# Mixer, MLP and routed experts on one core: expert rows added to the output by an accumulating scatter, and two splits of weights moved

## What is computed

```python
x = x + mixer_and_mlp(layernorm(x))          # first block
x = x + experts(layernorm(x))                # second block

def mixer_and_mlp(x):
    h  = x + mamba2(rmsnorm(x, ln1_w))       # in-projection 512 -> 2576, conv, scan, out-projection 1024 -> 512
    h2 = rmsnorm(h, ln2_w)
    return h + silu(h2 @ gate_w) * (h2 @ up_w) @ down_w     # 512 -> 2048 -> 512

def experts(x):                              # 8 experts, width 352, the 2 best of each row
    w, idx = top_k(softmax(x @ Wr), 2); w = w / w.sum()
    return sum(w[k] * (silu(x @ Wg[idx[k]]) * (x @ Wu[idx[k]])) @ Wd[idx[k]] for k in range(2))
```

## Time and profile before

| what | before |
|---|---|
| median of 3 executions | 1528.81 us (1527.99 to 1529.47) |
| the profiled execution, its own time | 1526.85 us |
| its span in the trace | 1525.1 us |
| TensorE busy | 1444.7 us, 95% |
| VectorE busy | 775.2 us, 51% |
| ScalarE busy | 446.2 us, 29% |
| GpSimd busy | 447.2 us, 29% |
| mean granted clock of TensorE | 0.985 of full |

### The profile page before, as it was taken

One profiled execution on the slowest core, in us unless ns is written; L12 is line 12 of the kernel. 1 busy time (PEld: TensorE's weight loads), 2 busy tenths in 40 slices (PEclk: granted clock), 3 DMA queues, 4 the chain that ended last, 5 costly groups with the idle time before them and its releaser, 6 DMA issues.

```text
span 1525.1 us, 19801 instructions
## 1 busy us (share of the span) xinstructions
PE 1444.7 (95%) x6871; PEld 1052.3 (69%) x6871; DVE 775.2 (51%) x1235; ACT 446.2 (29%) x926; POOL 447.2 (29%) x497
## 2 busy tenths in 40 slices
PE   6799999889999998999999999999988999999996
PEld 4577778556666666888888888888867555555553
DVE  6969778699999992333333332333465221211211
ACT  4444445455555552212112121211121111111110
POOL 2402121257777662101011010101012233333332
PEclk9999999899999998999999999999999999999998
DMA  9123123622332225010000001200476122222220
GB/s 195 56 104 105 68 83 133 206 90 105 117 119 98 98 71 193 28 28 29 14 28 28 14 28 28 97 7 12 148 244 232 57 77 79 87 87 84 81 64 17
DMA packets 84978, 130.97 MB, mean 86 GB/s; under 512 B 29213, under 2 KB 45597, under 8 KB 84896
## 3 DMA queue, kind: packets, MB, share of 16 engines
q1 hardware_dynamic: 71488, 103.62, 21.0%
q0 software_dynamic: 9360, 25.18, 5.4%
q10 hardware_dynamic: 4048, 1.10, 0.3%
HBM read 91.59 MB, written 43.78 MB: 89 GB/s over the span
## 4 chain that ended last, share of the span: by engine, by line
PE 38%; DMA 15%; issue 4%; DVE 3%; ACT 0%; POOLq 0%; POOL 0%; DVEq 0%; ACTq 0%
PE fin_bank L1744 35%; DMA result_rows<-out_dram,idx 8%; DMA out_dram<-result_rows,idx 7%; DVE result_rows L1729 2%; PE fin_bank L1885 1%; PE fin_bank L1854 1%; PE fin_bank L1867 0%; PE fin_bank L1812 0%; PE fin_bank L1800 0%; DMA xs<-xn_rows,idx 0%; DVE ff_w_lo L1581 0%; PE fin_bank L1903 0%; DVE fi_bn L1616 0%; ACT ff_w_hi L1505 0%; PE fin_bank L1810 0%
## 5 line engine op out<-in xcount | busy, mean ns | idle before, releaser
L1744 PE MATMUL fin_bank<-ff_hT_hi,ff_w_hi 128*128 128x512 f32 x512 | 203.0, 397 | 3.2 <-DVE ff_w_lo L1551 3.2
L1744 PE MATMUL fin_bank<-ff_hT_hi,ff_w_lo 128*128 128x512 f32 x512 | 202.7, 396 | 0.0
L1744 PE MATMUL fin_bank<-ff_hT_lo,ff_w_hi 128*128 128x512 f32 x512 | 202.7, 396 | 0.0
L1885 PE MATMUL fin_bank<-wx,xT 128*128 x624 | 192.9, 462 | 1.0 <-ACT xT L1520 0.8
L1543 DVE TENSOR_TENSOR ff_prod<-ff_prod,fin_bank 128x512 f32<-128x512 f32 x64 | 44.0, 688 | 263.8 <-PE fin_bank L1744 263.8
L1388 POOL TENSOR_TENSOR ff_w_lo<-ff_stage,ff_w_hi 128x1024 fp32r<-128x1024 f32 (+1 forms) x24 | 56.5, 2354 | 411.7 <-ACT ff_w_hi L1495 406.9
L1885 PEld LDWEIGHTS fin_bank<-wx,xT 128*128 128x128 f32 x624 | 116.4, 192 | 60.0 <-issue 2.7
L1729 DVE SCALAR_TENSOR_TENSOR result_rows<-fin_bank,wt,result_rows 128x512 f32<-128x512 f32 x39 | 29.3, 751 | 234.6 <-DMA result_rows<-out_dram,idx 232.1
L628 PE MATMUL pj_bank<-hT_hi,w_in_hi 128*128 128x512 f32 x336 | 135.7, 404 | 11.8 <-DVE zst L548 8.7
L530 DVE SCALAR_TENSOR_TENSOR conv_acc<-raw,conv_w,conv_acc 128x512 f32<-128x512 f32 x144 | 113.2, 786 | 42.6 <-ACT raw L339 35.1
L628 PE MATMUL pj_bank<-hT_lo,w_in_hi 128*128 128x512 f32 x336 | 133.9, 398 | 0.0
(11 more groups left out here) (264 smaller groups left out, 2455.0 us busy)
## 6 DMA issues: line engine op xcount, KB each, us to landing
cv_rows<-cst SPq DMA_DIRECT2D x12, 1024.0 KB, 4.2
cv<-cv_rows SPq DMA_DIRECT2D x16, 768.0 KB, 4.3
zs_rows<-zst SPq DMA_DIRECT2D x8, 1024.0 KB, 6.5
zs<-zs_rows SPq DMA_DIRECT2D x16, 512.0 KB, 5.3
wx<-in_L_ffn_Wg_dram SPq DMA_DIRECT2D x8, 704.0 KB, 8.4
wx<-in_L_ffn_Wu_dram SPq DMA_DIRECT2D x8, 704.0 KB, 9.0
w_raw<-in_L_attn_in_proj_w_dram SPq DMA_DIRECT2D x32, 128.0 KB, 3.8
x<-_attn_hidden_states_dram SPq DMA_DIRECT2D x16, 256.0 KB, 5.6
```

Of the source, the lines that this page charges most:

```text
L1744: mm = eng.matmul(ps, w[a], x[b], start=first and i == 0, stop=last and i == 2)
L1885: mm = eng.matmul(ps[:, 0:EI], xT[j % 2][:, k, :], wx[:, bass.ds(e, 1), at:at + EI].rearrange("p a n -> p (a n)"), start=(k == 0), stop=(k ...
```

## The change

There are three edits.

**Experts.** The old rows of the output are no longer read. VectorE only multiplies the result by the weight into one of two buffers `rows`, and one indirect DMA per tile adds it to the output in DRAM (`compute_op=ALU.add`). Such a DMA may not name a row twice, nor leave one to chance, so the empty slots of a tile now name real rows that the tile doesn't hold, and add zero to them. Their numbers come from a second list, `put_idx`. VectorE works it out in 17 small steps, two wide ones (`oj`) and two wider ones (`onehot`), TensorE makes another table from it with 16 one-hot products, which stand in its list between `turn_x(1)` and the first `turn_width`, and VectorE finishes it after `product(0)` (`put_list`). Each accumulating DMA waits for the one before it. GpSimd's list is now: three gathers, the wait for the list, and then for each tile one gather ahead, the wait for the result, the wait for the last accumulation, and the accumulating DMA.

**Table load.** ScalarE runs an exponential of one column before it waits for data, which brings the load of its function table forward. In the first loop of ScalarE and of VectorE the order is turned round: the transposed rows of k come before the weights of k.

**Out-projection split.** The eight and eight instructions that split `wo_raw` go in two halves into gaps of chunk 0: on ScalarE behind `exps(0, 1)` and `exps(0, 2)`, on VectorE behind `score(0, 1)` and `score(0, 3)`. TensorE's first out-projection waits for the first four, its second for the rest.

```diff
         eng.activation(neg_cum[:, g, :], dtb[:, UPG * HEADS:2 * UPG * HEADS], ACT.Copy)\
            .then_inc(s["cum_done"], 1)
+    eng.activation(sp[:, 2, 0:1], ones[:, 0:1], ACT.Exp)
     eng.wait_ge(s["ln1_dma"], 16)
+    turned(0, 0)
     for k in range(KD):
+        if k + 1 < KD:
+            turned(0, k + 1)
         if k == 0:
             eng.wait_ge(s["wa_dma"], 32)
         split(k, 0, W_C)
-        turned(0, k)
...
     rows_in(0)
     norm_rows(0)
+    turned(0, 0)
     for k in range(KD):
+        if k + 1 < KD:
+            turned(0, k + 1)
         split(k + 1, k, 0, W_C)
-        turned(0, k)
...
+    def out_high(lo, hi):
+        if lo == 0:
+            eng.wait_ge(s["v_dma"], 16 * 9)
+            eng.wait_ge(s["wo_dma"], 16 * 4)
+        for n in range(lo, hi):
+            eng.activation(wo_hi[:, n, :], wo_raw[:, n, :], ACT.Copy, scale=normw[:, n:n + 1])\
+               .then_inc(s["wo_hi"], 1)
...
             exps(c, 1)
+        if c == 0:
+            out_high(0, HPG)
         if late:
             high(e, 1)
         if now:
             exps(c, 2)
+        if c == 0:
+            out_high(HPG, NB)
...
-        if c == 0:
-            eng.wait_ge(s["v_dma"], 16 * 9)
-            eng.wait_ge(s["wo_dma"], 16 * 4)
-            for n in range(NB):
-                eng.activation(wo_hi[:, n, :], wo_raw[:, n, :], ACT.Copy, scale=normw[:, n:n + 1])\
-                   .then_inc(s["wo_hi"], 1)
...
+    def out_low(lo, hi):
+        for n in range(lo, hi):
+            eng.wait_ge(s["wo_hi"], n + 1)
+            eng.scalar_tensor_tensor(wo_lo[:, n, :], wo_raw[:, n, :], normw[:, n:n + 1],
+                                     wo_hi[:, n, :].bitcast(F32), ALU.mult, ALU.subtract).then_inc(s["wo_lo"], 1)
...
             score(c, 1)
+        if c == 0:
+            out_low(0, HPG)
         if late:
             low(e, 1)
...
             score(c, 3)
+            if c == 0:
+                out_low(HPG, NB)
             decayed_c(c, 1)
...
-        if c == 0:
-            for n in range(NB):
-                eng.wait_ge(s["wo_hi"], n + 1)
-                eng.scalar_tensor_tensor(wo_lo[:, n, :], wo_raw[:, n, :], normw[:, n:n + 1],
-                                         wo_hi[:, n, :].bitcast(F32), ALU.mult, ALU.subtract).then_inc(s["wo_lo"], 1)
...
-        if e == 0 and a == 0:
-            eng.wait_ge(s["wo_lo"], NB)
+        if e == 0:
+            eng.wait_ge(s["wo_lo"], HPG * (a + 1))
...
-    for t in xs + [rows]:
+    for t in xs:
         eng.memset(t[:, :], 0.0).then_inc(s["cleared"], 1)
-    eng.wait_ge(s["cleared"], UN + 1)
+    eng.wait_ge(s["cleared"], UN)
     eng.wait_ge(s["ids"], 1)
-    def at(j):
-        return bass.IndirectOffsetOnAxis(ap=idx[:, j:j + 1], axis=0)
     def gather(j):
         if j >= UN:
             eng.wait_ge(s["xT_ps"], j - UN + 1)
-        eng.indirect_dma_start(out=xs[j % UN][:, :], out_offset=None, in_=dr["xn"], in_offset=at(j),
+        eng.indirect_dma_start(out=xs[j % UN][:, :], out_offset=None, in_=dr["xn"],
+                               in_offset=bass.IndirectOffsetOnAxis(ap=idx[:, j:j + 1], axis=0),
                                bounds_check=ROWS - 1, oob_is_err=False).then_inc(xs_s[j % UN], 16)
-    gather(0)
-    gather(1)
+    for j in range(3):
+        gather(j)
     eng.wait_ge(s["out_dma"], 16 * NR)
+    eng.wait_ge(s["ids"], 3)
     for j in range(SORT_TILES):
-        ge(eng, s["put"], 16 * j)
-        eng.indirect_dma_start(out=rows[:, :], out_offset=None, in_=out_d, in_offset=at(j),
-                               bounds_check=ROWS - 1, oob_is_err=False).then_inc(s["got"], 16)
-        if j == 0:
-            gather(2)
         if j + 3 < SORT_TILES:
             gather(j + 3)
         eng.wait_ge(s["sum"], j + 1)
-        eng.indirect_dma_start(out=out_d, out_offset=at(j), in_=rows[:, :], in_offset=None,
-                               bounds_check=ROWS - 1, oob_is_err=False).then_inc(s["put"], 16)
+        ge(eng, s["put"], 16 * j)
+        eng.indirect_dma_start(out=out_d, out_offset=bass.IndirectOffsetOnAxis(ap=put_idx[:, j:j + 1], axis=0),
+                               in_=rows[j % 2][:, :], in_offset=None, bounds_check=ROWS - 1,
+                               compute_op=ALU.add).then_inc(s["put"], 16)
     eng.wait_ge(s["put"], 16 * SORT_TILES)
...
+    def both_tiles(a):
+        return a.unsqueeze(1).broadcast_to([P, 2, E])
+    last_t, first_pad = pad_e[:, 0, :], pad_e[:, 1, :]
+    behind, member, at_slot, free = (pad_q[:, i, :, :] for i in range(4))
+    row_of = rowm[:, 1, 0:2].unsqueeze(2).broadcast_to([P, 2, E])
+    step(eng.scalar_tensor_tensor(last_t, ends[:, 1, :], -1.0, ends[:, 2, :], ALU.add, ALU.max))
+    step(eng.scalar_tensor_tensor(first_pad, ends[:, 2, :], float(P), a[:, pad + TILES - 1, :], ALU.mult, ALU.add))
+    step(eng.scalar_tensor_tensor(behind, both_tiles(last_t), -float(P), sc[:, 0:2, :], ALU.mult, ALU.add))
+    step(eng.scalar_tensor_tensor(member, behind, 0.0, hot[:, 0:2, :], ALU.is_ge, ALU.mult))
+    step(eng.scalar_tensor_tensor(at_slot, behind, 0.0, row_of, ALU.max, ALU.subtract))
+    step(eng.tensor_tensor(at_slot, both_tiles(first_pad), at_slot, ALU.subtract))
+    step(eng.tensor_scalar(at_slot, at_slot, float(ROWS), None, ALU.add))
+    step(eng.scalar_tensor_tensor(free, both_tiles(ends[:, 1, :]), float(P), at_slot, ALU.mult, ALU.is_gt))
+    step(eng.tensor_tensor(free, free, member, ALU.is_gt))
+    step(eng.scalar_tensor_tensor(at_slot, at_slot, 1.0, free, ALU.add, ALU.mult))
+    step(eng.tensor_scalar(at_slot, at_slot, -1.0, None, ALU.add))
+    step(eng.tensor_scalar(behind, at_slot, 1.0 / P, -0.49609375, ALU.mult, ALU.add))
+    step(eng.tensor_scalar(behind, behind, big, None, ALU.add))
+    step(eng.tensor_scalar(behind, behind, -big, None, ALU.add))
+    step(eng.scalar_tensor_tensor(member, behind, -float(P), at_slot, ALU.mult, ALU.add))
+    step(eng.tensor_scalar(pad_j[:, :], iota_q[:, 1, 0:SORT_TILES], ends[:, 1, E - 1:E], rowm[:, 1, 0:1],
+                           ALU.is_ge, ALU.mult))
+    step(eng.tensor_tensor(pad_j[:, :], table_ps[:, 0:SORT_TILES], pad_j[:, :], ALU.add))
+    NP = 2 * E
+    step(eng.tensor_tensor(oj[:, 0:NP, 0, :], iota_q[:, 1, 0:SORT_TILES].unsqueeze(1).broadcast_to([P, NP, SORT_TILES]),
+                           behind.rearrange("p t e -> p (t e)").unsqueeze(2).broadcast_to([P, NP, SORT_TILES]),
+                           ALU.is_equal))
+    eng.tensor_tensor(oj[:, 0:NP, 0, :].rearrange("p (t e) j -> p t e j", t=2),
+                      oj[:, 0:NP, 0, :].rearrange("p (t e) j -> p t e j", t=2),
+                      rowm[:, 1, 0:2].unsqueeze(2).unsqueeze(3).broadcast_to([P, 2, E, SORT_TILES]), ALU.mult)\
+       .then_inc(s["onehot"], 1)
+    for t in range(2):
+        eng.tensor_tensor(onehot[:, t * E:(t + 1) * E, :], iota_q[:, 1, 0:P].unsqueeze(1).broadcast_to([P, E, P]),
+                          member[:, t, :].unsqueeze(2).broadcast_to([P, E, P]), ALU.is_equal).then_inc(s["onehot"], 1)
+    def put_list():
+        eng.wait_ge(s["table"], 2)
+        step(eng.tensor_tensor(pad_j[:, :], table_ps[:, 0:SORT_TILES], pad_j[:, :], ALU.add))
+        eng.tensor_scalar(put_idx[:, :], pad_j[:, :], float(ROWS), None, ALU.add).then_inc(s["ids"], 1)
...
     def weighted(j):
         eng.wait_ge(s["y_ps"], j + 1)
-        eng.wait_ge(s["got"], j * 16 + 16)
-        eng.scalar_tensor_tensor(rows[:, :], y_ps[j % 2][:, :], wt[:, j:j + 1], rows[:, :], ALU.mult, ALU.add)\
-           .then_inc(s["sum"], 1)
+        ge(eng, s["put"], 16 * (j - 1))
+        eng.tensor_scalar(rows[j % 2][:, :], y_ps[j % 2][:, :], wt[:, j:j + 1], None, ALU.mult).then_inc(s["sum"], 1)
     product(0)
+    put_list()
     for j in range(SORT_TILES):
...
         eng.wait_ge(s["hT"], j + 1)
+        if j == 1:
+            eng.wait_ge(s["ids"], 3)
         ge(eng, s["sum"], j - 1)
...
     turn_x(1)
+    eng.wait_ge(s["onehot"], 9)
+    eng.wait_ge(s["ids"], 2)
+    for n in range(2 * E):
+        last = eng.matmul(table_ps[:, 0:SORT_TILES], onehot[:, n, :], oj[:, n, 0, :], start=(n == 0), stop=(n == 2 * E - 1))
+    last.then_inc(s["table"], 1)
...
-        [("result_rows", [P, D], F32)])
+        [(f"result_rows{i}", [P, D], F32) for i in range(2)])
```

More of the change, by code:

```diff
@@ L1262, in finish @@
         (iota_q, rowm, e8, tri8, strict, half_neg, lgT, sums_a, sums_b, lg, ex, sc, hot12, hot, cmp_n, cmp_t, red, wk, ends,
-         slot, wsum, idx, wt, te_f, tile_expert) = lay["small"]
+         slot, wsum, idx, wt, te_f, tile_expert, put_idx, pad_e, pad_q, pad_j) = lay["small"]
         onehot, oj, act_g0, act_g1, hT_e = lay["table"]
-        xs, xT, rows = lay["rows"][0:UN], lay["rows"][UN:UN + 2], lay["rows"][UN + 2]
+        xs, xT, rows = lay["rows"][0:UN], lay["rows"][UN:UN + 2], lay["rows"][UN + 2:UN + 4]
         act_g = [act_g0, act_g1]
@@ L1272, in finish @@
             "counts", "onehot", "table", "ids", "cleared",
```

(5 more changed lines are left out.)

## The result

The changed kernel takes **1515.69 us** (median of 4 executions, 1515.05 to 1516.31), the kernel before, on the same chip, 1529.14 us (1527.99 to 1531.31). The ratio is 0.9913 with a 95% interval of 0.9900 to 0.9926, so it is faster, by 13.5 us. The forecast of 1505.5 us was 10.2 us too low, and the time lies 1.7 us above the end of its range. The profiled execution took 1515.05 us, with a span of 1513.3 us where the forecast had 1501.8 us. So the trace has 11.5 us to account for.

The account below looks back on a forecast made before the run. The ring of row reads and writes was taken as the bound at 8.66 us a tile, TensorE next at 8.08. Experts 20.1 + table load 1.4 + split 1.8 = 23.3 us off gave 1505.5 us, range 1500.5 to 1514.

Parts of the forecast that it names:

- The pace: Experts: without the read of old rows, TensorE becomes the bound at 8.08 us a tile, from the ring's 8.66 us.
- The second list: Experts, before the first tile: VectorE's 7.5 us hidden in idle time, TensorE's 16 products 3.6 us with nothing beside them.
- rival on the ring: Experts: accumulating DMA above 8.0 us issue to issue sets the pace, chance 0.06; above 8.48 us, slower than before, 0.07.
- The gathers didn't starve: Rival, experts' start: GpSimd held until VectorE's list is made, first tile 6.8 us late, time 1512.3 us; chance 0.07.
- the tail of the new end: Experts' end: 3.89 us from last write's issue to span end, as before, plus 1.5 us for the accumulation.
- The early edits, 1.4 + 1.8 us: Before the experts: table load 1.4 us and out-projection split 1.8 us gained; rival that they give nothing, 1508.7 us, chance 0.08.
- Table load: Mixer's start: load at about 10.5 us, VectorE's last split ending at about 19.75 instead of 21.41, gain 1.4 us.
- Split: Chunk 0's out-projection split: gain 1.8 us, bounds 0.5 and 2.7, with `carried(0, 1)` starting about 2 us later.
- its lower bound of 0: Table load's gain bounded from 0, where a weight load ends late and takes it all, to 1.7 us.
- The last two tiles: Experts' end: from `turn_width(38)` at 1494.01, 1.27 us transposes and copies, 2.78 `down`, 1.58 to the DMA's issue at 1499.64.
- The upper bound of the pace: Experts: accumulation adding at most 3.5 us makes the ring's turn 7.0 us, under TensorE's 8.08 us.
- The price of the accumulation: Experts' accumulating DMA: 1.5 us more than a plain write of about 3.5 us, bounds nothing and 3.5 us.

Follow-up runs that it names:

- f4_no_list: The changed kernel with scatters by the first list, empty slots skipped, and the second list's computation, products and waits deleted: 1508.91 us, ratio 0.9873 against the kernel before.
- g4_out_late: The changed kernel with the second half of the out-projection's low parts on VectorE moved behind chunk 0's row norms: 1513.00 us, ratio 0.9894 against the kernel before.
- g3_warm_only: The changed kernel with 9 and 6 more idle TensorE products, warm(12) to warm(21) and warm(14) to warm(20): 1512.99 us, ratio 0.9890 against the kernel before.
- e3_plain_put: The changed kernel with a scatter that writes plainly and doesn't add, second list kept: 1512.66 us, ratio 0.9892 against the kernel before.
- f1_put_36: The changed kernel without the accumulating scatters of tiles 36, 37 and 38, empty with this input: 1503.32 us, ratio 0.9834 against the kernel before.
- f2_extra_39: The changed kernel with 39 more small indirect gathers on GpSimd's queue: 1511.21 us, ratio 0.9887 against the kernel before.
- e4_skip_empty: The changed kernel with accumulating scatters by the first list, empty slots skipped, second list still made: 1512.03 us, ratio 0.9890 against the kernel before.

## Why the prediction was right and wrong, by its steps

**Right.**
- The pace: 8.08 us a tile, set by TensorE, and the waits name TensorE and the result.
- The second list: VectorE's part from 1171.83 to 1179.5 us, hidden. TensorE's 3.66 us, of which the forecast had 3.2 net on the path (1184.22 to 1187.40) and `f4_no_list` shows 3.1.
- Neither rival on the ring came: one accumulating scatter took 5.33 us from its issue to the next when the two stood one behind the other, far under 8.08 us. The gathers didn't starve. The issues of the first three took 1.33, 1.02 and 1.63 us while VectorE made its list. The third is 0.6 us longer than without the list (1.00 in `f4_no_list`), and nothing waited for it.
- The direction, and the place of the table load.

**Wrong: 11.5 us of span in the profiled execution, in four terms.**

1. *"The last write before is issued at 1521.21 and the span ends at 1525.1, 3.89 us later"*, used as the tail of the new end with 1.5 us on top. This is the step that failed: 5.9 us. The tail was taken as one piece from one row. It holds three things: the landing, GpSimd's drain, and 0.2 us. The drain grew by 5.06 us, and the forecast had no term for it. It goes with GpSimd's list of DMAs, which is another. The landing grew by 2.35 us, of which 1.5 was forecast.
2. *The early edits, 1.4 + 1.8 us*: 0.70 us were left at `lgT` (1144.79 before, 1144.09 after), 2.5 us too few. One execution is a draw here too. The 12 profiled executions with both edits as changed come to `lgT` between 1141.87 and 1144.14 us, the three with neither between 1143.34 and 1145.10, and the means are 1.0 us apart. In detail:
   - *Table load.* The forecast step happened: the load is at 10.70 us and VectorE's last split ends at 20.06 us in place of 21.41. The lead was 2.0 us at the third pre-activation (30.77 against 32.79). Then ScalarE came to weights that hadn't landed and waited 2.91 us, and the next one is at 36.51 us in place of 35.57. Behind it TensorE waits 4.17 us for GpSimd's low parts, 1.16 us before. A lead came back with the stall that ends at 63.57 (before 64.49), and was gone at 72.72 (72.39 before). The forecast named this, "a weight load ends late and takes it all", as its lower bound of 0 and argued past it from VectorE's later stall. The first product of the state-space part is 0.31 us later than before (287.78 against 287.47).
   - *Split.* The forecast saw that the second half delays `carried(0, 1)` by 2 us and took it to be harmless. It was 2.7 us (304.10 to 306.77), TensorE's clock fell to 0.60 and 0.54 in the two stretches of 4 us from 304 on, and the gain was gone. `g4_out_late` shows that 1.8 us were to be had.
3. *The clock between router and table*, 1.6 us: the sum took the durations of one execution as fixed, and that execution was one of the 3 in 15 with the full clock. `g3_warm_only` shows the cost.
4. *The last two tiles*, 1.4 us, from `turn_width(38)` at 1494.93 to the last issue at 1502.00, 7.07 us where the forecast had 5.63. Tile 38 has no `wide` ahead of it, so its result is there after 4.3 us and not 8.08, and the accumulating scatter of tile 37 needs 5.33 us. GpSimd waits 3.78 us for it, and 1.0 us of the 1.4 is this. The other 0.4 us are in the transposes, copies and hand-offs ahead of the result. The upper bound of the pace was compared with 8.08 us, and not with the shorter last turn. With a plain scatter or with skipped slots this wait is gone.

These are 5.9 + 2.5 + 1.6 + 1.4 = 11.4 us of the 11.5.

**The price of the accumulation.** A plain write of the earlier trace rows took 2.77 us, the accumulating one of the last chain 4.50 us: 1.7 us more, where 1.5 was taken. Over all tiles the medians are 2.8 us (the same in `e3_plain_put`, which writes all 128 rows) and 4.8 us, 2.0 us more. Its issue takes 1.59 us of GpSimd in place of 1.03. The Trainium skill ("Collectives: The Full Stack", section "The bandwidth ceiling: the fold count and why AG ≠ RS ≠ AR") has a reducing stream 1.93 times slower, which as an estimate from that page would be 5.3 us; here the factor is 4.50 / 2.77 = 1.62, and 1.7 by the medians. On this price the page was a little high and the bounds from the rows held.

**Shown and not shown.** That the drain is GpSimd's own, and that it costs 5.06 us more than before, is shown by the records and by `f1_put_36`. That its length goes with the list of DMAs is shown by `f2_extra_39` and the runs beside it. The second list's 3.1 us, the clock and the split's second half have an experiment each. That late weights eat the table load's lead is read from the waits and not tried by itself. What sets the drain's length, and what decides whether the clock falls in a gap of 2.3 us, is open.

## What to carry to other kernels

A tail (the time from the last issue to the end) copied from the old trace is only good for the old list of instructions. Take it apart (landing, drain, barrier) and ask of each part what the change does to it, above all when the change alters what GpSimd issues. The last turns of a pipeline are shorter than its steady ones, so compare a bound with the shortest turn too. And one profiled execution holds draws of TensorE's clock: where an idle gap stands ahead of a row of dense products, price both clock levels, or fill the gap.

## What the runs showed of the hardware that was not expected

- GpSimd's closing drain took between 1.38 and 7.51 us, repeatable to 0.01 us for the same list of indirect DMAs, and 39 more DMAs made it 4.1 us shorter. It counts in the time if GpSimd ends last. In `f1_put_36`, where it began more than 14 us ahead of the end, it cost nothing.
- An accumulating scatter of 128 rows of 2 KB: 1.59 us of GpSimd's issue (1.03 plain), 4.5 to 5.1 us to its landing, 4.8 in the median (2.8 plain), and 5.33 us from issue to issue when one waits for the other.
- The accumulating scatter also skips indices outside the rows (`e4_skip_empty`, `f4_no_list`). The change was built as if it could not. The list of pad rows wasn't needed, and leaving it out was worth 3.1 us.
- With an idle gap of 2.3 us ahead of dense products the granted clock fell in 12 of 15 profiled executions; with one of 0.3 us in none of 3.
